# Reordering VectorE's work in the second half of a group norm and attention kernel

## The reference

```python
xn = group_norm(x, gamma, beta)          # 32 groups, EPS = 0.001
xf = xn.reshape(B, N, C)                 # B = 16, N = 1024, C = 512
q = xf @ wq + bq
k = xf @ wk + bk
v = xf @ wv + bv
scores = jnp.einsum('bnc,bmc->bnm', q, k) * C ** (-0.5)
attn = jax.nn.softmax(scores, axis=-1)
out = jnp.einsum('bnm,bmc->bnc', attn, v)
out = out @ wp + bp
return out.reshape(B, H, W, C) + residual
```

## Time and profile before

| | us |
|---|---|
| median of 3 runs | 2138.52 (2137.93 to 3012.9) |
| the profiled execution's own time | 2139.97 |
| span in its profile, first to last instruction | 2138.3 |
| TensorE busy | 2099.0 (98%) |
| VectorE busy | 1798.7 (84%) |
| GpSimd busy | 877.3 (41%) |
| ScalarE busy | 743.7 (35%) |

### The profile page before, as it was taken

How to read it: one execution, slowest core, us unless ns; L and a number is a source line. 1 busy time by engine, 2 the same in 40 slices (tenths; PEclk the granted TensorE clock), 3 DMA queues, 4 the chain that set the end, 5 groups by cost and what they waited for, 6 DMA issues and landing times.

```text
span 2138.3 us, 28427 instructions
## 1 busy us (share of the span) xinstructions
PE 2099.0 (98%) x9253; PEld 1730.9 (81%) x9253; DVE 1798.7 (84%) x2554; ACT 743.7 (35%) x1216; POOL 877.3 (41%) x475
## 2 busy tenths in 40 slices
PE   7999999999999999999999999999999999999999
PEld 5877888888888888888888788888878888888887
DVE  6898897988979888888888979889788898888865
ACT  4242332423333243332523324233332433335232
POOL 2452442524335244443524425243352434435253
PEclk9999999999999999999999999999999999999999
DMA  8003012030300203012030120303012030120101
GB/s 211 20 11 109 1 54 64 15 103 0 94 24 34 83 0 118 0 49 69 10 108 0 56 62 15 103 0 93 25 34 83 0 118 0 49 69 10 69 1 60
DMA packets 110268, 108.13 MB, mean 51 GB/s; under 512 B 8476, under 2 KB 74016, under 8 KB 110240
## 3 DMA queue, kind: packets, MB, share of 16 engines
q1 hardware_dynamic: 107984, 103.58, 16.0%
q10 hardware_dynamic: 2256, 4.20, 0.8%
HBM read 74.19 MB, written 33.55 MB: 50 GB/s over the span
## 4 chain that ended last, share of the span: by engine, by line
PE 51%; DVE 19%; issue 18%; POOL 7%; ACT 3%; DMA 0%; POOLq 0%; DVEq 0%; ACTq 0%
PE psum L1226 6%; PE psum L1228 6%; PE psum L1227 6%; PE psum L1251 5%; PE psum L1253 5%; PE psum L1252 5%; PE psum L1140 4%; PE psum L1139 4%; PE psum L1137 4%; DVE pt_lo L694 4%; POOL total_part L449 4%; DVE score L869 3%; DVE xn_lo L694 3%; POOL total_part L458 2%; PE psum L1057 2%
## 5 line engine op out<-in xcount | busy, mean ns | idle before, releaser
L1251 PE MATMUL psum<-v_hi,pt_hi 128*128 128x512 f32 x1024 | 401.4, 392 | 20.6 <-DVE pt_lo L694 17.4
L426 POOL TENSOR_TENSOR x_res<-x_res,out_bias 128x512 f32<-128x512 f32 x128 | 201.8, 1600 | 499.1 <-PE psum L1140 371.4
L1252 PE MATMUL psum<-v_lo,pt_hi 128*128 128x512 f32 x1024 | 399.2, 390 | 0.0
L1253 PE MATMUL psum<-v_hi,pt_lo 128*128 128x512 f32 x1024 | 399.0, 390 | 0.0
L694 DVE TENSOR_TENSOR pt_lo<-score,pt_hi 128x512 fp32r<-128x512 f32 x256 | 295.2, 1178 | 28.3 <-POOL total_part L449 25.0
L449 POOL TENSOR_TENSOR total_part<-total_part,score 128x512 f32<-128x512 f32 x192 | 309.1, 1610 | 16.6
L592 ACT ACTIVATE score<-psum 128x512 f32<-128x512 f32 x256 | 152.5, 596 | 342.3 <-PE psum L1228 341.9
L1251 PEld LDWEIGHTS psum<-v_hi,pt_hi 128*128 128x128 f32 x1024 | 192.6, 188 | 68.5 <-DVE pt_lo L694 25.1
L1253 PEld LDWEIGHTS psum<-v_hi,pt_lo 128*128 128x128 f32 x1024 | 192.6, 188 | 40.3
L1252 PEld LDWEIGHTS psum<-v_lo,pt_hi 128*128 128x128 f32 x1024 | 192.7, 188 | 39.1
L1226 PE MATMUL psum<-v_hi,xn_hi 128*128 128x512 f32 x512 | 201.7, 394 | 0.0
(11 more groups left out here) (162 smaller groups left out, 3992.2 us busy)
## 6 DMA issues: line engine op xcount, KB each, us to landing
x_res<-in_x_dram SPq DMA_DIRECT2D x128, 256.0 KB, 3.0
out_dram<-x_res SPq DMA_DIRECT2D x128, 256.0 KB, 2.2
x_blk<-in_x_dram SPq DMA_DIRECT2D x240, 128.0 KB, 3.2
score<-in_x_dram SPq DMA_DIRECT2D x16, 128.0 KB, 8.0
w_q<-in_L_conv_wq_dram SPq DMA_DIRECT2D x1, 1024.0 KB, 5.5
w_k<-in_L_conv_wk_dram SPq DMA_DIRECT2D x1, 1024.0 KB, 7.9
w_v<-in_L_conv_wv_dram ACTq DMA_DIRECT2D x1, 1024.0 KB, 9.1
w_p<-in_L_conv_wp_dram ACTq DMA_DIRECT2D x1, 1024.0 KB, 13.0
```

The source lines that it names most:

```text
L426: last = nc.gpsimd.tensor_tensor(at, at, out_bias[:, first:end], ALU.add)
L1251: nc.tensor.matmul(dst, hi[:, m, queries], v_hi[:, m, :], start=m == 0, stop=False)
L1252: nc.tensor.matmul(dst, hi[:, m, queries], v_lo[:, m, :], start=False, stop=False)
L1253: end = nc.tensor.matmul(dst, lo[:, m, queries], v_hi[:, m, :], start=False, stop=m == NT - 1)
```

## The change

Six edits, all of order but one:

- VectorE's totals of the first half move from in front of V tile 7's low part to behind the eight subtractions of the second shift.
- In the second half, each pair of `pt_lo` is followed by its output tile, and the four `xn_lo` of the next image come together behind them. Output tile 0 thus moves behind the first pair.
- The variance of the next image moves from behind the loop over the second half's maxima into it, at m = 6.
- In image 0 the residuals 0 to 3 are made by VectorE (`first_residual`) instead of GpSimd.
- In image 0 the low parts of four block sums of A (`block_lo`) move from between V tiles 4 and 5 to behind the output tiles 4 to 7.
- TensorE's wait for these low parts moves from behind image 0 into `queries`, ahead of S2.

```diff
@@ GpSimd
                 top(b, 1)
-                if starts(b):
-                    for i in range(TH):
-                        residual(b, i)
                 totals(b, 1)
@@ VectorE
+            def first_residual(i):
+
+                dve.wait_ge(s_bias, BIAS_STEPS)
+                dve.wait_ge(s_xr[i], 16)
+                at = x_res[:, i, :]
+                nc.vector.tensor_tensor(at, at, out_bias[:], ALU.add).then_inc(s_res, 1)
...
                     if more and m == 3:
                         group_variance(b + 1)
+                    if more and m == 6:
+                        variance(b + 1)
                     if m > 1:
                         pt_lo_parts(b, 0, m - 2, m - 1)
-                if more:
-                    variance(b + 1)
                 pt_lo_parts(b, 0, NT - 2, NT)
                 for m in range(2, NT - 1):
                     v_lo_part(b, m)
                     if more and m == 4:
                         norm(b + 1)
-                    if starts(b) and m == 4:
-                        for n, at in enumerate(SUMS):
-                            block_lo(at, len(WHOLE) + n + 1, ab_sum[:, at])
-                totals(b, 0)
                 v_lo_part(b, NT - 1)
                 tile_shift(b, 1)
                 shifts(b, 1, 0, NT)
-                tile_out(b, 0)
+                totals(b, 0)
+                if starts(b):
+                    for i in range(TH):
+                        first_residual(i)
+
                 for j in range(KC):
                     pt_lo_parts(b, 1, 2 * j, 2 * j + 2)
-                    if more:
-                        xn_lo_parts(b + 1, j, j + 1)
-                    if j:
-                        tile_out(b, j)
+                    tile_out(b, j)
+                if more:
+                    xn_lo_parts(b + 1, 0, KC)
...
                         sum_lo_part(b + 1, i - TH)
+                    if starts(b):
+                        block_lo(SUMS[i - TH], len(WHOLE) + i - TH + 1, ab_sum[:, SUMS[i - TH]])
@@ TensorE
+                        pe.wait_ge(s_abl, len(WHOLE) + len(SUMS))
                         pe.wait_ge(s_xsl, earlier(n) * 4 + 1)
...
                 image(0, True)
-
-                pe.wait_ge(s_abl, len(WHOLE) + len(SUMS))
```

## The result

The changed kernel takes 2229.18 us (median of 4 runs, 2228.54 to 2235.32) against 2138.64 for the kernel before: ratio 1.043, 95% interval 1.0416 to 1.0445. It is slower by 90.5 us. One of the four runs of the kernel before took 3012.9 us; the ratio and its interval leave it out. The forecast was 2212 in a range of 2190 to 2240.

The account below looks back on a forecast made before the run. TensorE was taken as the bound. Profiled 2139.97 us + 75 (5.35 us in each of 14 loop images) - 1 (image 0) = 2214; the runs' median is 1.45 lower, so 2212 us, range 2190 to 2240.

Parts of the forecast that it names:

- The mechanism: Loop images: GpSimd's program swap starts only once VectorE writes the reciprocals; moved totals uncover it, first addition 6.7 us later.
- Rival 1: GpSimd's configuration is not held back by the reciprocals, so the swap stays covered: 2120 us, chance 0.09.
- The size of the swap: GpSimd in loop images: from the reciprocal's start to the first addition 7.60 us in the mean.
- The reciprocal: VectorE, image 14: first-half reciprocal at +8.67 us after the first output product, instead of +1.88.
- the chain on VectorE: Image 14, after first output product: pt_lo from +17.7 to +30.6 us, V tile 0 split at +59.6, S3 at +59.9.
- Where TensorE waits: Per loop image: 4.3 us at the fifth output tile, 2.55 at product S3 (needs V tile 0 split), 6.85 together.
- I put it at 0: Sooner variance: GpSimd's reduction beside the next input's norm on VectorE costs 0, give or take 0.3 us an image.
- rival 2: TensorE's granted clock falls once an image behind the stalls: +24 us, 2236 us, chance 0.11.
- Image 0: Wait of 3.12 us before outputs goes, 4 to 6 us before image 1's S2 comes: -1 us, between -4 and +3.
- Image 15: Last image: no effect, its swap is hidden and 2 us of slack remain at its pt_lo.

Follow-up runs that it names:

- e3: Changed kernel plus a small GpSimd sum into a spare tile ahead of its wait for the second half's reciprocals: 2139.93 us, ratio 1.0009.
- e1: Changed kernel with VectorE's first-half totals back in front of V tile 7's low part: 2139.36 us, ratio 1.0008.
- e2: Kernel before with only the totals moved behind the eight subtractions of the second shift: 2249.24 us, ratio 1.0524.
- e13: Kernel before with the regrouping, and the totals between the shift's two operations and the eight subtractions: 2158.97 us, ratio 1.0081.
- e5: Kernel before with the sooner variance alone: 2140.38 us, ratio 1.0012.
- e6: Changed kernel with the variance back behind the loop: 2230.33 us, ratio 1.0436.
- e9: Changed kernel with totals in front of V tile 7 and the variance back behind the loop: 2118.68 us, ratio 0.9909.
- e8: Changed kernel with a small GpSimd sum ahead of the wait for the reciprocals and the variance back: 2119.38 us, ratio 0.9911.

## Why the prediction was right

*The mechanism* was as put: by the order of the program, a configuration behind the wait, and a swap that the reciprocals start. Run e3 shows it with nothing else changed, e1 and e2 from both sides, e13 by degree. Rival 1, that the swap stays covered, is refuted by 2052.5 beside 2043.87.

*The size of the swap* was 7.60, and 7.46 came. The reciprocal was put at +8.67; counted from where the outputs would have started without their new wait (2044.55 - 1.32, which is the distance of matmul starts less 0.2267), it came at +8.9. Counted so, the chain on VectorE came as forecast. In image 14 the second half's `pt_lo` began at +17.8 (forecast +17.7), the last of them ended at +30.4 (forecast +30.6), and S3 started at +59.3 (forecast +59.9).

*Where TensorE waits* was wrong in its shares. I had 4.3 at the fifth output tile and 2.55 at S3, 6.85 together. It was 2.3 there (in distances of starts), 2.2 at S3, and 1.3 in front of the outputs, 5.8 together, with some 0.5 in gaps too short for a wait. Whatever TensorE loses early it doesn't lose at the fifth tile, since the chain on VectorE sets when the fifth tile and S3 can go on. So the sum came close (6.3 against 6.85) though its parts did not: the wait in front of the outputs was not in it at all, and the one at the fifth tile was shorter by 2.0 us.

*The step that failed* is "I put it at 0" on the variance. I had the sum of totals hit the norm once, for 2 us, under the cover of the last `v_hi`. The sum of totals came not 1.8 but 2.5 us sooner (5.8 us ahead of the outputs' unhindered start, against 3.2 before), and the second reduction follows it at once, so both lie beside the norm. The norm took 6.12 instead of 2.98 us, 3.1 more, and V tile 6, which TensorE needs in front of its outputs, comes 1.2 us late. e5 shows the wait with this edit alone. With the swap uncovered the edit made no difference that the runs tell from their spread (e6), but without that swap it would have hidden the gain of the regrouping: 2139 with it (e1, e3) and 2118 or 2119 without (e9, e8).

*The clock* was rival 2, at 0.11, and it came, in addition. The forecast time left it out. The change took 17 us more than the forecast, and this accounts for all of it: in 12 of the 14 loop images matmuls follow each other at 0.43 us for a while behind the wait at S3, and in image 7 behind the wait in front of the outputs too. In image 4 of the changed kernel:

```profile
740.52 0.49 PE L1142 MATMUL psum<-xs_hi,ab_hi 128*128 128x512 f32 x1 [2.10 <-DVE v_lo L691]
...
742.39 0.63 PE L1144 MATMUL psum<-xs_lo,ab_hi 128*128 128x512 f32 x1
742.81 0.63 PE L1145 MATMUL psum<-xs_hi,ab_lo 128*128 128x512 f32 x1
743.24 0.63 PE L1142 MATMUL psum<-xs_hi,ab_hi 128*128 128x512 f32 x1
```

Some eight steps longer by 0.2 us make 1.6 us an image, some 20 us in all. Without them the time would have been about 2209 us, an estimate. The measured time lies in the range because the range took this rival as its upper end, not because the forecast had the clock right. Image 5, where the clock did not fall, against image 4 shows the price apart: the periods from outputs 5 to 6 and from 4 to 5 are 134.78 and 136.24 us. (Image 6, where it did not fall either, takes 135.93 us, with a wait of 1.82 instead of 1.16 us in front of the next outputs.)

*Image 0* was put at -1 us. The wait at S2 for the low parts of A, which I had at 4 to 6 us, is 5.07, and 1.58 of the 3.12 in front of the outputs have stayed, because of the lengthened norm. From outputs 0 to 1 the trace has 136.78 us against 132.32, but outputs 0 begin at 137.00 instead of 140.84: 0.6 us slower up to image 1, inside the bound of -4 to +3. *Image 15* showed nothing, as said.

## What to carry to other kernels

A program swap on GpSimd (here 6.7 to 7.7 us from the configuration to the first addition behind a reduction, in the loop images before and after) is issued where its configuration stands in the order; in a device loop, a wait written ahead of the first operation can land ahead of the configuration, and then the swap starts only when the wait ends. Look at where MODIFY_POOL_CONFIG stands against the signal before you move the signal's producer, and put a small operation of the new kind ahead of the wait if the wait must be late: that gave back 89 us here with one line. And test edits one by one: the regrouping alone is worth 20 to 23 us (ratio 0.9909 and 0.9895), and two other edits of the same change each hid it (e1 and e6).

## What was not expected of the hardware

The granted clock fell behind shorter idles than the trace before suggested. Behind S3 in image 4 (740.52, above) and in image 5 (876.92) of the changed kernel stand like idles and unlike clocks (windows below, columns as in the earlier trace rows):

```profile
876.92 0.49 PE L1142 MATMUL psum<-xs_hi,ab_hi 128*128 128x512 f32 x1 [2.11 <-DVE v_lo L691]
...
877.20:883.00 5.80, 5.80 (x27) 4.74 (x27) 4.49 (x8) 1.27 (x2) 0.00 (x0) 1.00 1.02 287
742.10:745.40 3.30, 3.30 (x10) 2.52 (x9) 1.44 (x3) 0.00 (x0) 0.00 (x0) 0.50 1.04 289
```

The clock is 0.50, the 1.2 GHz level, behind an idle of 2.10 us in the one and 1.00, the 2.4 GHz level, behind 2.11 in the other, as it was behind 2.95 in the earlier trace rows. In image 7 it fell to 0.50 behind 1.82. In e13 it fell behind each of the seven waits of 1.90 to 2.14 us at S3 and behind none of the seven of 1.27 to 1.81. So the length of the idle alone does not decide it; what does was not tried.

GpSimd's reductions and VectorE's norm were both slower where they ran side by side. In image 14 of the changed kernel the four operations of the norm took 6.12 instead of 2.98 us, and the two reductions 3.76 and 2.73 instead of 3.25 and 1.88. With the variance back (e6) the norm and the reductions lie one behind the other, and it is 2.98, 3.25 and 1.88 again.
